# A graph network kernel's opening stage: one more fold in split form, with small work handed to GpSimd

## The reference, cut to what matters

```
h = relu(layernorm(x));  x = x + L0(h)      # edge network
h = relu(layernorm(x));  x = x + L1(h)      # three layers of mean aggregation
h = relu(layernorm(x));  x = x + L2(h)      # one graph convolution
h = relu(layernorm(x));  x = x + L3(h)      # three convolutions, joined

L0: msg = (silu(edge @ We1 + be1) @ We2 + be2) * h[dst]
    agg = segment_sum(msg, src);  h + silu(agg @ Wn1 + bn1) @ Wn2 + bn2
L1: h = relu(h @ W_init.T), then for l in 0..2:
    fwd = mean_agg(h, src, dst) @ W_fwd[l].T
    bwd = mean_agg(h, dst, src) @ W_bwd[l].T
    h = relu(concat(h, fwd, bwd) @ W_self[l].T)
```

## Time and profile before

| | |
|---|---|
| median of 3 runs | 1156.27 us (1155.58 to 1157.21) |
| profiled execution | 1155.25 us |
| its span | 1153.5 us |
| PE busy | 1135.2 us, 98% |
| DVE busy | 848.1 us, 74% |
| ACT busy | 666.3 us, 58% |
| POOL busy | 406.4 us, 35% |
| mean granted TensorE clock | 0.997 of full |

### The profile page before, as it was taken

One profiled execution on the slowest core, in us unless ns is written; L12 is line 12 of the kernel. 1 busy time (PEld: TensorE's weight loads), 2 busy tenths in 40 slices (PEclk: granted clock), 3 DMA queues, 4 the chain that ended last, 5 costly groups with the idle time before them and its releaser, 6 DMA issues.

```text
span 1153.5 us, 20475 instructions
## 1 busy us (share of the span) xinstructions
PE 1135.2 (98%) x6097; PEld 952.3 (83%) x6097; DVE 848.1 (74%) x1485; ACT 666.3 (58%) x1351; POOL 406.4 (35%) x536
## 2 busy tenths in 40 slices
PE   9999999999999999999999999999999999999998
PEld 5677888888888888888888888888889788898786
DVE  9995788877777777777777777877888234177665
ACT  2666666767676767676766767676734123141362
POOL 2005565555565555555554555552000000002000
PEclk9999999999999999999999999999999999999999
DMA  8743522222222222222222222222101102022101
GB/s 253 290 151 123 210 87 72 86 73 83 76 76 83 79 81 77 82 71 87 70 89 70 86 73 80 79 76 52 47 1 68 43 20 89 0 74 73 46 1 46
DMA packets 27830, 95.86 MB, mean 83 GB/s; under 512 B 6629, under 2 KB 6879, under 8 KB 23698
## 3 DMA queue, kind: packets, MB, share of 16 engines
q0 software_dynamic: 18592, 54.42, 15.7%
q1 hardware_dynamic: 9072, 40.84, 10.2%
q10 hardware_dynamic: 130, 0.13, 0.1%
HBM read 86.52 MB, written 8.85 MB: 83 GB/s over the span
## 4 chain that ended last, share of the span: by engine, by line
PE 90%; DVE 6%; ACT 2%; issue 1%; DMA 0%; POOL 0%; DVEq 0%; ACTq 0%; POOLq 0%
PE ps L1026 13%; PE ps L1027 13%; PE ps L1028 13%; PE ps L1019 10%; PE ps L1020 9%; PE ps L1021 9%; PE ps L1034 3%; PE ps L1033 3%; PE ps L1124 3%; PE ps L1123 3%; PE ps L1128 2%; PE ps L1141 1%; PE ps L1284 1%; DVE ended L1638 1%; PE ps L1063 1%; DVE hot_hi L1632 1%
## 5 line engine op out<-in xcount | busy, mean ns | idle before, releaser
L1026 PE MATMUL ps<-we_hi,s_hi 128*128 128x512 f32 x664 | 267.4, 403 | 0.0
L1027 PE MATMUL ps<-we_lo,s_hi 128*128 128x512 f32 x664 | 259.8, 391 | 0.0
L1028 PE MATMUL ps<-we_hi,s_lo 128*128 128x512 f32 x664 | 259.7, 391 | 0.0
L599 POOL DMA_INDIRECT xg<-h_dram,node_picks x166 | 175.4, 1056 | 96.7 <-POOL node_picks L589 65.3
L737 ACT ACTIVATE m_hi<-msg 128x512 fp32r<-128x512 f32 x166 | 105.0, 632 | 168.2 <-DVE msg L1744 93.2
L593 POOL DMA_INDIRECT rbf<-in_edge,edge_picks x166 | 173.0, 1042 | 50.5 <-issue 36.3
L1749 DVE TENSOR_TENSOR m_lo<-msg,m_hi 128x512 fp32r<-128x512 f32 x166 | 115.0, 693 | 60.0 <-ACT m_hi L737 60.0
L1737 DVE TENSOR_TENSOR s_lo<-s,s_hi 128x1024 fp32r<-128x1024 f32 x83 | 101.7, 1225 | 69.2 <-ACT s_hi L731 45.2
L1028 PEld LDWEIGHTS ps<-we_hi,s_lo 128*128 128x128 f32 x664 | 124.7, 188 | 27.4
L1026 PEld LDWEIGHTS ps<-we_hi,s_hi 128*128 128x128 f32 x664 | 125.0, 188 | 21.4
L1027 PEld LDWEIGHTS ps<-we_lo,s_hi 128*128 128x128 f32 x664 | 125.3, 189 | 20.6
(11 more groups left out here) (307 smaller groups left out, 2440.1 us busy)
## 6 DMA issues: line engine op xcount, KB each, us to landing
fold_dram<-folded SPq DMA_DIRECT2D x6, 1024.0 KB, 5.3
wstage<-fold_dram SPq DMA_DIRECT2D x6, 1024.0 KB, 4.9
stage<-in_fold_a SPq DMA_DIRECT2D x3, 1024.0 KB, 16.6
stage<-in_fold_b SPq DMA_DIRECT2D x3, 1024.0 KB, 24.0
w_raw<-in_nodew SPq DMA_DIRECT2D x3, 1024.0 KB, 7.5
wstage<-in_selfw SPq DMA_DIRECT2D x3, 1024.0 KB, 5.0
rbf<-in_edge,edge_picks POOLq DMA_INDIRECT x166
xg<-h_dram,node_picks POOLq DMA_INDIRECT x166
```

The lines of the kernel that those rows point to most:

```text
L599: pool.indirect_dma_start(xg[t.slot][:, j], None, h_dram, bass.IndirectOffsetOnAxis(ap=node_picks[t.slot][:, j:j + 1], axis=0)).then_inc(x ...
L1026: pe.matmul(outp, lh, rh, start=False, stop=False, skip_group_check=True)
L1027: pe.matmul(outp, lh, rl, start=False, stop=False, skip_group_check=True)
L1028: return pe.matmul(outp, ll, rh, start=False, stop=False, skip_group_check=True)
```

## The change

Only the opening stage changes.

- Fold 2 is in split form too (`WHOLE = 2`, `BY_POOL = 2`). Its high parts are made by ScalarE, two quarters behind each of the units (1,2) and (1,3) in its order; its low parts by GpSimd. Its stage and parts use buffer set 0, so SyncE loads fold 4's factors only when GpSimd's low parts are done.
- The bucket tables are made by GpSimd, behind its constants, in 22 steps, each of which waits for the one before; a compare with add in one instruction becomes two instructions. VectorE waits for the last of them (`BUCKET_STEPS`) where it first uses them, behind the slot tables.
- The row statistics stand behind unit (3,3), which is behind the last one-hots, and the norm behind unit (4,0), on VectorE and ScalarE.
- SyncE loads the factors of folds 1, 2 and 3 ahead of `x`, and saves `h` behind the products 2 and 3.
- The first four gathers of edge rows take their columns straight from `slot_edge` and start at `table_ready` 1. The copies into `edge_picks` begin with step 2.

```diff
-WHOLE = 3
+WHOLE = 2
+BY_POOL = 2
+BUCKET_STEPS = 4 * C + 2
...
-            load_factors(1)
+            for m in range(1, FOLDS - 2):
+                load_factors(m)
             sp.dma_start(x_res[:], a["x"].rearrange("(c p) f -> p c f", p=NC)).then_inc(x_in, 16)
-            for m in range(2, FOLDS - 1):
-                load_factors(m)
...
+            sp.wait_ge(pool_split_lo, K)
+            load_factors(FOLDS - 2)
             save_product(1)
             sp.wait_ge(split_lo, K)
             load_factors(FOLDS - 1)
-            sp.wait_ge(ln_act, 1 + C)
-            sp.dma_start(h_dram.rearrange("(c p) f -> p c f", p=NC), h32[:]).then_inc(h_saved, 16)
             for m in range(2, FOLDS):
+                if m == FOLDS - 2:
+                    sp.wait_ge(ln_act, 1 + C)
+                    sp.dma_start(h_dram.rearrange("(c p) f -> p c f", p=NC), h32[:]).then_inc(h_saved, 16)
                 save_product(m)
...   (GpSimd)
+            def then(ins):
+                counted[0] += 1
+                ins.then_inc(bucket_step, 1)
+                pool.wait_ge(bucket_step, counted[0])
+
+            pool.wait_ge(halved, 5)
+            pool.wait_ge(bounds_known, 1)
+            then(pool.tensor_scalar(pairs_end[:], upto[:, 0], 2.0, None, ALU.mult))
+            then(pool.tensor_scalar(solo_tile[:], solo_at[:], 1.0 / P, None, ALU.mult))
+            then(pool.tensor_scalar(solo_end[:], upto[:, 1], solo_tile[:, 0:1], None, ALU.add))
+            then(pool.tensor_scalar(bucket_f[0][:], tile_no[:], solo_tile[:, 0:1], float(1 - C), ALU.is_ge, ALU.mult))
+            for i, end_at in enumerate(ends):
+                then(pool.tensor_scalar(tile_base[:], tile_no[:], end_at, None, ALU.is_ge))
+                then(pool.tensor_tensor(bucket_f[(i + 1) % 2][:], tile_base[:], bucket_f[i % 2][:], op=ALU.add))
+            bucket = bucket_f[len(ends) % 2]
+            then(pool.tensor_scalar(tile_base[:], bucket[:], float(NC), -1.0, ALU.mult, ALU.add))
+            then(pool.tensor_copy(bucket_row[:], bucket[0:1]))
+            for k in range(K):
+                pool.wait_ge(split_hi, k + 1)
+                pool.tensor_tensor(fold_lo[0][:, :, k], stage[0][:, :, k], fold_hi[0][:, :, k],
+                                   op=ALU.subtract).then_inc(pool_split_lo, 1)
+            pool.wait_ge(table_ready, 1)
+            for c in range(2):
+                for j in range(2):
+                    pool.indirect_dma_start(
+                        rbf[c][:, j], None, a["edge"],
+                        bass.IndirectOffsetOnAxis(ap=slot_edge[:, 2 * c + j:2 * c + j + 1], axis=0)).then_inc(rbf_in[c], 16)
             pool.wait_ge(table_ready, 2)
             pool.wait_ge(h_saved, 16)
...
-            for c in range(2):
-                pick_edges(Step(None, c))
             pick_nodes(Step(None, 0))
-            pool.wait_ge(picked, 3)
-            gather_edges(Step(None, 0))
-            gather_edges(Step(None, 1))
+            pool.wait_ge(picked, 1)
             gather_nodes(Step(None, 0))
...   (ScalarE)
-                if WHOLE <= m + 1 < FOLDS:
+                if BY_POOL < m + 1 < FOLDS:
                     factor_high(m + 1, u)
+                if m + 1 == BY_POOL and u >= K // 2:
+                    for k in range(2 * u - K, 2 * u - K + 2):
+                        factor_high(BY_POOL, k)
...
-                if (m, u) == (2, 1):
+                if (m, u) == (4, 0):
                     norm()
...   (TensorE, fold)
+                    if u == 0 and m == BY_POOL:
+                        pe.wait_ge(pool_split_lo, k + 1)
+                    elif u == 0:
+                        pe.wait_ge(split_lo, (m - BY_POOL - 1) * K + k + 1)
...   (VectorE)
-                if (m, u) == (2, 2):
-                    bucket_tables()
...
-                if (m, u) == (1, 3):
+                if (m, u) == (3, 3):
                     dve.wait_ge(x_in, 16)
                     for c in range(C):
                         row_stats(c)
-                if (m, u) == (2, 1):
+                if (m, u) == (4, 0):
                     norm()
...
             dve.wait_ge(perm_out, 9)
+            dve.wait_ge(bucket_step, BUCKET_STEPS)
```

More of the change, by code:

```diff
@@ L310, in build @@
         assert spare.at <= keep.at
-        plain_at = (spare.at - 2 * 2 * K * F * 4, spare.at - 2 * K * F * 4, pre.at - 2 * 2 * K * F * 4)
+        plain_at = (spare.at - 2 * 2 * K * F * 4, spare.at - 2 * K * F * 4)
         plain = [Region(at)(f"plain{m}", [P, 2, K, F], F32) for m, at in enumerate(plain_at)]
@@ L434, in build @@
         stage_in = [sem(f"stage_in{m}") for m in range(FOLDS)]
-        split_hi, split_lo = sem("split_hi"), sem("split_lo")
+        split_hi, split_lo, pool_split_lo = sem("split_hi"), sem("split_lo"), sem("pool_split_lo")
         fold_mm, fold_ev = sem("fold_mm"), sem("fold_ev")
@@ L440, in build @@
             sem("perm_zeroed"), sem("hots_lo_made"), sem("hots_hi_made"), sem("marks_made"), sem("perm_mm"))
-        halved = sem("halved")
+        halved, bounds_known, bucket_step = sem("halved"), sem("bounds_known"), sem("bucket_step")
         perm_out, pos_ready, halves_made = sem("perm_out"), sem("pos_ready"), sem("halves_made")
@@ L578, in _ @@
             pool.memset(ones[:].bitcast(F32), 1.0).then_inc(consts_ready, 1)
+            counted = [0]
+            def then(ins):
[8 more added lines that the diff above has]
+            then(pool.tensor_scalar(bucket_f[0][:], tile_no[:], solo_tile[:, 0:1], float(1 - C), ALU.is_ge, ALU.mult))
+            ends = [pairs_end[:, b:b + 1] for b in range(C - 1)] + [solo_end[:, b:b + 1] for b in range(C - 1)]
+            for i, end_at in enumerate(ends):
[14 more added lines that the diff above has]
+                        bass.IndirectOffsetOnAxis(ap=slot_edge[:, 2 * c + j:2 * c + j + 1], axis=0)).then_inc(rbf_in[c], 16)
             pool.wait_ge(table_ready, 2)
@@ L601, in gather_nodes @@
                         bass.IndirectOffsetOnAxis(ap=node_picks[t.slot][:, j:j + 1], axis=0)).then_inc(xg_in[t.slot], 16)
-            for c in range(2):
-                pick_edges(Step(None, c))
             pick_nodes(Step(None, 0))
-            pool.wait_ge(picked, 3)
-            gather_edges(Step(None, 0))
-            gather_edges(Step(None, 1))
+            pool.wait_ge(picked, 1)
             gather_nodes(Step(None, 0))
             pick_edges(Step(None, 2))
-            pool.wait_ge(picked, 4)
+            pool.wait_ge(picked, 2)
             gather_edges(Step(None, 2))
@@ L621, in edge_step @@
                     pick_nodes(t.at(1))
-                    pool.wait_ge(picked, t.count(2, 6) if within(3) else t.c + STEPS + 2)
+                    pool.wait_ge(picked, t.count(2, 4) if within(3) else t.c + STEPS)
                     pool.sem_inc(picks_landed, 1)
@@ L693, in factor_high @@
                 act.wait_ge(stage_in[m], 32)
-                act.wait_ge(fold_mm, K * (m - 1))
+                if m > BY_POOL:
+                    act.wait_ge(fold_mm, K * (m - 1))
                 act.activation(fold_hi[m % 2][:, :, k], stage[m % 2][:, :, k], ACT.Copy).then_inc(split_hi, 1)
@@ L1065, in fold @@
                         continue
-                    if u == 0:
-                        pe.wait_ge(split_lo, (m - WHOLE) * K + k + 1)
+                    if u == 0 and m == BY_POOL:
+                        pe.wait_ge(pool_split_lo, k + 1)
+                    elif u == 0:
+                        pe.wait_ge(split_lo, (m - BY_POOL - 1) * K + k + 1)
                     hi, lo = fold_hi[m % 2], fold_lo[m % 2]
@@ L1589, in _ @@
             dve.wait_ge(halved, 5)
+            dve.sem_inc(bounds_known, 1)
             dve.tensor_scalar(jump[1][:], jump[0][:], solo_at[:, 0:1], None, ALU.add).then_inc(halved, 1)
@@ L1651, in weights_low @@
                     dve.tensor_tensor(low[:], raw[:], high[:], op=ALU.subtract).then_inc(weights_lo, 1)
[L1653 to L1666, removed]
             def slot_tables():
@@ L1693, in _ @@
             for n, (m, u) in enumerate(units):
-                if u == K - 1 and WHOLE <= m + 1 < FOLDS:
+                if u == K - 1 and BY_POOL < m + 1 < FOLDS:
                     factor_low(m + 1, u)
@@ L1700, in _ @@
                     slot_tables()
-                if (m, u) == (2, 2):
-                    bucket_tables()
-                if u < K - 1 and WHOLE <= m + 1 < FOLDS:
+                if u < K - 1 and BY_POOL < m + 1 < FOLDS:
                     factor_low(m + 1, u)
-                if (m, u) == (1, 3):
+                if (m, u) == (3, 3):
                     dve.wait_ge(x_in, 16)
```

## The result

| | before | after |
|---|---|---|
| median | 1156.17 us (4 runs, 1155.58 to 1157.21) | 1165.71 us (4 runs, 1164.73 to 1165.94) |
| profiled execution | 1155.25 us | 1165.68 us |
| its span | 1153.5 us | 1163.9 us |
| PE busy | 1135.2 us | 1137.5 us |
| POOL busy | 406.4 us | 440.7 us |

The changed kernel takes 1.0081 times as long, 95% interval 1.0068 to 1.0094. The forecast was 1162.3 us, slower, with a range from 1151.0 to 1169; the likeliest case was "held as forecast", with a range of its own from 1158.7 to 1166.

The account below looks back on a forecast made before the run. VectorE's one-hots, held by GpSimd, were taken to bound the opening: 93.9 + 17.3 = 111.2 us for the first edge-row transpose, 6.0 later than 105.24; 1156.3 + 6.0 = 1162.3 us, range 1151.0 to 1169.

Parts of the forecast that it names:

- held as forecast: Likeliest case: GpSimd's reads hold VectorE's one-hots for 13.5 us, ending at 1162.3 us; chance 0.48.
- Held by GpSimd: VectorE's one-hots lose 13.5 us to GpSimd's SBUF reads: 5.1 to table steps, 8.4 to four low halves.
- One sign: Expected in the trace: one-hot sets beside table steps at over 2.3 us a pair instead of 1.77.
- Rivals 1: Opening stage: GpSimd and VectorE run side by side, transpose at 101.4, 1152.5 us; chance 0.26.
- 2: VectorE held for less, 6.7 us, transpose at 104.4, 1155.5 us; chance 0.16 together with Rival 4.
- Rival 3: VectorE held longer, a low 3.7 us, and the norm's table load not hidden: 1169 us; chance 0.10.
- Rival 4: A gather ends the transpose's wait at T + 12.5: 1157.5 us, 1148 at best; 0.16 shared with rival 2.
- T: End of VectorE's last one-hots: 80.4 for VectorE alone plus 13.5 lost to GpSimd, 93.9 us; before, 90.3.
- TensorE's ring: Ring of four one-hot sets: VectorE makes one only when the place four earlier is done; TensorE's side gives T = 84.1.
- Fold 2 on TensorE: Split units save 2.5 us, but fold 2 waits until GpSimd's fourth low near 51; overlaps VectorE's loss, not added.
- Behind T: VectorE and ScalarE chain from last one-hot to first edge-row transpose, statistics through fold (5,0): 17.3 us, before 14.9.
- Moves I cost at nothing: SyncE's reordered loads and later save of h (5 to 6 us transfer): no cost, 10 us of cover.

Follow-up runs that it names:

- run 2: Changed kernel with fold 2's four low halves made by VectorE instead of GpSimd, tables staying on GpSimd: 1162.48 us, 1.0045 of the kernel before.
- run 8: The probe: kernel before plus nine GpSimd operations with unused results (three subtractions, three fills, three copies) beside the one-hots: 1163.65 us, 1.0059.
- run 3: Changed kernel with row statistics and norm back at their old places, behind units (1,3) and (2,1): 1168.08 us, 1.0101 of the kernel before.
- run 4: Changed kernel with low halves and bucket tables on VectorE (tables behind the rows' first low part), statistics and norm at old places: 1163.28 us, 1.0042 of before.
- run 6: Kernel before with the bucket tables still on VectorE but behind the rows' first low part: 1155.64 us, 0.9988.
- run 7: Kernel before with tables late on VectorE and first four edge-row gathers straight from the sorted table: 1152.88 us, 0.9966; repeated 1152.54, 0.9961.
- Run 5: Kernel before with only the first four gathers of edge rows taken straight from the sorted table: 1153.72 us, 0.9975.
- run 9: Run 7's kernel with the first norm's five ReLUs spread over ScalarE's units (2,2) to (3,2): 1160.18 us, 1.0029 of the kernel before.
- run 10: Kernel before with only the first norm's five ReLUs spread over ScalarE's units of folds 2 and 3: 1163.15 us, 1.0058.
- run 11: Run 9's kernel with SyncE's save of h behind the save of product 2 instead of in front: 1152.32 us, 0.9964 of the kernel before.
- run 1: Changed kernel with the bucket tables back on VectorE behind unit (2,2), fold 2's low halves staying on GpSimd: 1165.93 us, 1.0081 of the kernel before.

## Why the prediction was right

**Held by GpSimd (13.5 forecast).** Twelve sets of one-hots cost 6 x 2.00 + 6 x 1.53 = 21.2 us alone; they began at 20.76 and ended at 54.7, so 12.8 were lost. The tables took 3.9 of it up to 42.27 (forecast 5.1): a compare stretches a one-hot by 0.12 (0.79 for 0.67), an add by 0.34 (0.90 for 0.55), where I had 0.16 and 0.40. The rest is 8.9 (forecast 8.4 for the lows), of which the last two table steps have 0.25: four one-hots are about 2.2 longer each. The mechanism was right, and its two sizes erred in opposite directions. One sign came out weaker than written: the ten sets beside the tables took 2.15 us each on average, not over 2.3. Rivals 1 and 2 are out: their losses were 1 and 6.7, and runs 2 and 8 show the same hold with GpSimd's lows taken away and with nothing but GpSimd's reads put in. Rival 3 is out too: a low lasted 2.67 us, not 3.7, and the norm's table load (97.02) was hidden. (Its own sum, 1162.3 + 6 + 1.3, is 1169.6, not 1169.) Rival 4 fell with the transpose, which waited for fold 5 and no gather.

**T (93.9 forecast, 94.6 measured).** 80.4 + 12.8 = 93.2; another 1.23 is the wait for a high half of ScalarE at 69.99, and 0.17 the later start of the one-hots (20.76 against 20.59), together 94.6. That T came within 0.7 is partly luck: the hold was 0.7 less than forecast, and the wait was not in the sum. I had counted TensorE's ring as VectorE's only other limit. Here the slip is small, but it is the step that failed in my later expectations: runs 3, 4, 6 and 7 each met 3.6 us of it.

**Fold 2 on TensorE.** GpSimd's tables took until 43.1, not 38, since a step lasts until the one-hot beside it is through: a compare 1.27, an add 0.55 or 1.01. So the lows ran from 43.2 to 53.8, not 40 to 51, and TensorE stood 5.4 us at unit (2,0); the stretch from 50 to 65 has a clock of 0.77. As forecast this lay beside VectorE's loss: VectorE never waited for TensorE behind it.

**Behind T (17.3 forecast, 18.3 measured).** The chain over VectorE and ScalarE came as written, in the same order: the ReLUs from 99.93, `weights_high` from 104.91, the last low half at 110.22 for 1.2. The last quarter of fold (5,0), from 111.51, then took 1.43 us and not 0.71: its matmuls are 0.78 and 0.63 long, as in the row at 110.07, against 0.39 where the clock is 1.00. TensorE had idled 1.07 and 2.79 before. That is 0.7 of the 1.0; the rest are steps of 0.1.

**The gathers** were forecast as worth nothing here and were: slot_edge was there at 100.8, the first gather at 101.14, and the transpose had no wait. Run 5 shows that they are worth 2 us where they are last.

**The save of h** was undersized: 13.27 us in the chain of waits, not 5 to 6.

```profile
103.61 13.27 DMA h_dram<-h
```

So the node rows, forecast for near 117, were only asked for at 117.67, with the first message at 129.55. No row shows a wait for them; the cover of 10 us paid for it. But the later gathers of edge rows stand behind them on GpSimd, and TensorE did wait for the fourth step's:

```profile
136.59 0.33 PE L1114 MATMUL ps<-ident,rbf 128*128 128x128 f32 x1 [1.07 <-DMA rbf<-in_edge,edge_picks]
```

The chain of waits of the changed kernel runs over the save of `h` and this row, yet the wait cost nothing: the first four steps took 35.4 us as before. In run 4 the same wait was 2.48 and did cost. "Moves I cost at nothing" came out right here with less room than it had reckoned.

**Sum (1161.3 forecast for the profiled execution, 1165.68 measured).** +0.7 is T, +1.0 the tail, +0.7 the clock up to the first message. That is 2.4 of the 4.4; 1.65 more came in the loop, where I had assumed that the shift of the transpose is the shift of the end, and 0.3 behind it. A step of the loop takes 8.28 us on average at first in both kernels. Later it takes 8.35 in the kernel before, from about the 36th step on, and 8.37 in the changed one, from about the 26th on; the earlier turn and the longer step make about half of the 1.65 each. The operations are no longer than before it (`msg` 0.68 us, second-layer matmuls 0.39 to 0.40), and the clock is 1.00. From the first message to the last it took 686.2 us; before 684.5, runs 5, 7 and 8 684.6, run 3 684.9, runs 6, 9, 10 and 11 685.8 to 685.9, run 1 686.4, run 2 686.5, run 4 687.8. What sets the turn stays open; it doesn't follow the loop's start (run 3 has its first message at 131.99, the latest of all, and is among the short ones). That it is DMA traffic, or the phase of GpSimd's gathers, was not tried. Nor is it shown that the change causes it: each of these loops is one execution, and 22 executions of the kernel before, beside runs 5 to 8, lie between 1155.3 and 1158.8 us.

## What to carry to other kernels

Work handed to GpSimd is not off VectorE if it reads SBUF while VectorE's operations have two inputs there: the low halves cost VectorE 8.9 us from GpSimd and 4.5 in its own program. Fills cost VectorE nothing. A GpSimd operation that read 1024 columns cost VectorE 0.6 to 0.8 of its own length (2.2 of 2.67 us, 1.5 to 1.7 of 2.1 to 2.2), a small one 0.12 to 0.34 us, and GpSimd itself waited up to one VectorE operation at each. And before taking work off a busy engine, look at what the engine would wait for in its place: 5 us of tables taken away made T 1.2 sooner, while a gather that ended TensorE's wait made the transpose its whole 2 us sooner. And a save moved back can hold work that stands behind its reader: here the gathers of edge rows.

## What the runs showed of the hardware

- The hold's size, by GpSimd's operation: 0.12 us for one input of 166 columns, 0.34 for two; 0.84 for one input of 1024, 1.5 to 2.2 for two; none for a fill of 4096 (3.51 us). The Trainium skill (page "SBUF — State Buffer", section "Who interferes with whom") has each block the other; the traces agree for both sides, of which the kernel before showed VectorE's at 0.03 to 0.04 us only, and the hold was shorter than the other engine's operation (2.2 of 2.67 us).
- In the probe the first subtraction took 9.58 us and the others 2.09 and 2.21, the first copy 6.33 and the others 1.04 and 1.32; the one-hots ran untouched until 37.2, so the first 8 us held nothing. The first ones are 7.4 and 5.1 longer than the middle ones of the others. The Trainium skill (page "GPSIMD Engine Reference", section "2.1 Instruction dispatch") tells of a costly first call, and the trace agrees in kind. In the changed kernel the first two-input operation took 0.55; why is open.
- After idle times of 2.2 to 2.8 us TensorE's clock fell to its lower level (1.2 of 2.4 GHz) for some microseconds: in the changed kernel matmuls that take 0.39 took 0.63 up to 114.65, with a mean clock of 0.87 from 112.94 to 121 and of 1.00 from there; the mean was 0.79 in run 6 (104 to 112), run 8 (108 to 116) and run 4 (132 to 140), and 1.00 in the 8 us behind each. In the kernel before, an idle of 2.20 was followed by 1.00. What tells them apart is open.
- A save of 1250 KB from 125 partitions took 13.3 us in the changed kernel and 15.9 in runs 3 and 4. Put ahead of another save in SyncE's queue it cost ScalarE 7.94 us in run 9, and with the two swapped (run 11) nothing.
